# W_dec turned into contiguous tiles on chip, a new order of the setup, and splits in place in PSUM

## The chip, the cores and the metric

The kernel runs on one core of a Trainium2 chip. The metric is the device time of one execution in microseconds, the median of several runs. A core has five engines with a queue each: TensorE (PE in the profile, with its weight loads as PEld), VectorE (DVE), ScalarE (ACT), GpSimd (POOL) and SyncE (SP), which here only issues DMAs. Engines wait for each other through semaphores, and each works through its own list strictly in order.

## What is computed

Four conditioned layers, each added to its input, over x of 128 entries x 64 positions x 256 features in fp32 (cut to what matters):

```python
# layer 0: a weight per entry, decoded from its condition
U = (cond @ W_dec + b_dec).reshape(128, 257, 30)      # W_dec is 128 x 7710
x = x + (x @ (U[:, :-1] @ V) + U[:, -1] @ V)
# layer 1: modulated, demodulated product
s = cond @ (affine_w / sqrt(128)).T + affine_b
x = x + clip(((x * s) @ weight.T) * rsqrt(sum((weight * s)**2) + 1e-8) + bias, -256, 256)
# layer 2: adapter with weights made from the condition
x = x + (x + relu(x @ (down * dg + db)) @ (up * ug + ub))
# layer 3: norms with gains by class, three small nets, and an integration net
h = ln(ln(x, pw[id]), cp[id]);  t = ln(x, tm[id]);  s = ln(x, ms[id])
m, n, r = (x + ln(silu(c @ W1 + b1) @ W2 + b2) * g + be for c in three_conditions)
x = x + ln(silu(concat(softmax(aw) * [h, t, m, n, r, s]) @ int_W1 + b1) @ int_W2 + b2)
```

## The kernel before

**Setup.** The decode makes U: pe_dec (L447) runs 60 matmuls in 16 groups of four or two (GROUPS). Each takes one of the 30 columns r for 128 rows i out of wdec, whose elements lie in the order (i, r), so its weights are strided by 30 elements. v_decode (L542) adds b_dec and writes u_all. Six PSUM banks (dec_bank) serve in turn. pe_tail and v_ubias make the bias part, split it into three bf16 pieces, and act_ubwrite (L627) writes them to a scratch in DRAM, from which load_ub reads each chunk's part. pe_style, pe_dc, v_dceps, act_sqrt, v_dcrcp and g_dcoef make layer 1's coefficients. The three nets are pe_hid, act_hid (SiLU), pe_mo, v_mostat, g_moroot, v_monorm, pe_mot. pe_row and pe_cls then take them and the class biases through int_W1, and v_rows (L600) and v_classes (L606) split the results into bf16 pieces, all in SBUF; v_classes also picks each row's piece with masks. The loads of nets_W2, nets_rows and int_W1 reuse wdec and wait for the decode's last matmul.

**Main part.** Sixteen chunks of 512 positions (8 entries). For chunk c the stages are: act_u, pe_t, act_th1, act_th2, pe_x1, v_x1add (layer 0); g_style, pe_l1, v_l1mul, v_l1min, v_x2add (layer 1); pe_dn, v_dnmul, v_dnadd, act_relu, g_wup, pe_up, v_x3sum (layer 2, x3); pe_x3r, v_xstat, g_rootx, act_xnorm, pe_xht, act_xht (the norm); pe_tm, pe_ms, pe_cp with v_tmprod, v_msprod, v_hprod (gains by class); pe_shift and pe_w1_x3, _tm, _ms, _h (integration, in split precision), act_silu, act_silh, v_sillow, pe_w2, and the last norm v_ystat, v_ycentre, v_ynorm and store.

**Order.** Each engine has a list of (stage, chunk) written out by hand: begin, then a loop of ten rounds whose stages have fixed distances in chunks, then end. In the loop a round holds the integration of one chunk and the early layers of later ones:

```python
    for stage, n in begin:
        stage(eng, chunk(n))
    with eng.Fori(fill // 2, NCH // 2) as i:
        for k in range(2):
            for stage, lag in order:
```

The begin lists of before end ahead of chunk 0's pe_shift; the loop does the integration of chunks 0 to 9 and the end lists that of 10 to 15.

## Time and profile before

| | |
|---|---|
| median of 3 runs | 574.19 us (571.29 to 574.43) |
| the profiled execution: its own time | 574.62 us |
| its span, first to last instruction | 572.4 us |
| PE busy | 507.2 us, 89% |
| DVE, POOL, ACT busy | 80%, 69%, 52% |
| mean granted TensorE clock | 0.962 |

Times within a trace are us from the span's start. PE's granted clock is given as a share of 2.4 GHz; 0.50 is 1.2 GHz. A busy share over the whole span mixes the setup, the loop and the end, which have different limits.

### The profile page before, as it was taken

Reading aid. Unit: us, or ns where it says so; the run is one execution under the profiler, and the core shown is the slowest. Engines: PE = TensorE matmul, PEld = TensorE weight load, DVE = VectorE, ACT = ScalarE, POOL = GpSimd, SP = SyncE. Lnnn points to the kernel's source line nnn. Section 1 sums busy time; section 2 is a strip of 40 time slices with the busy share of each in tenths; the row PEclk is TensorE's granted clock in tenths of the full one; section 3 lists DMA queues with packets and bytes.
Section 4 is the critical chain, followed back from the end, with each engine's and each line's share of the span. In section 5 each row is a group of like instructions: output and inputs, shape, how many; then the busy total and the mean of one; then the engine's idle time right before and its main releaser. Section 6 shows DMA issues by size and latency. Waiting matters only on the chain.

```text
span 572.4 us, 8901 instructions
## 1 busy us (share of the span) xinstructions
PE 507.2 (89%) x2960; PEld 373.3 (65%) x2960; DVE 457.0 (80%) x857; ACT 299.6 (52%) x470; POOL 393.9 (69%) x382
## 2 busy tenths in 40 slices
PE   2996594699998999999999998999898999999873
PEld 2994252456767777677767776777666777778663
DVE  1444779768987898989898988898997989898833
ACT  0026424566647484848484848483746483656420
POOL 7601769288786788868886887688865897875320
PEclk9998787799998999999999999999999999999996
DMA  8338664033180808080908090908091505113011
GB/s 299 125 87 260 152 197 109 18 97 78 44 184 12 212 0 224 0 224 0 224 0 224 0 222 3 223 2 218 7 223 41 167 22 151 38 42 112 0 37 38
DMA packets 34955, 61.76 MB, mean 108 GB/s; under 512 B 4985, under 2 KB 17381, under 8 KB 34548
## 3 DMA queue, kind: packets, MB, share of 16 engines
q1 hardware_dynamic: 28868, 44.11, 28.5%
q0 software_dynamic: 5344, 16.87, 11.1%
q10 hardware_dynamic: 720, 0.48, 0.3%
q8 instruction: 13, 0.21, 0.2%
q14 instruction: 10, 0.08, 0.0%
HBM read 52.58 MB, written 8.87 MB: 107 GB/s over the span
## 4 chain that ended last, share of the span: by engine, by line
PE 60%; DMA 11%; DVE 9%; POOL 6%; issue 6%; SPq 3%; ACT 3%; POOLq 0%; DVEq 0%; ACTq 0%
PE ps_c L816 8%; PE ps_c L818 8%; PE ps_c L817 7%; DMA idx_ch<-in_mask 6%; PE ps_d L860 5%; PE ps_d L872 4%; PE ps_a L884 3%; PE ps_b L816 2%; PE ps_b L817 2%; PE ps_b L818 2%; DMA x_t<-in_x_t 2%; PE ps_a L456 2%; PE ps_b L902 2%; PE ps_c L456 2%; PE ps_a L902 2%
## 5 line engine op out<-in xcount | busy, mean ns | idle before, releaser
L1312 POOL DMA_INDIRECT pw_rows<-in_pw,gidx x64 | 71.2, 1112 | 27.9 <-issue 14.0
L860 PE MATMUL ps_d<-xm_t,l_w 128*128 128x512 f32 x128 | 60.9, 619 | 6.5 <-POOL xm_t L1321 6.5
L1321 POOL TENSOR_TENSOR xm_t<-x_t,style 128x1024 f32<-128x1024 f32 x16 | 30.5, 1905 | 38.8 <-DVE x_t L1163 38.8
L860 PEld LDWEIGHTS ps_d<-xm_t,l_w 128*128 128x128 f32 x128 | 23.8, 196 | 33.0 <-issue 30.7
L1350 POOL TENSOR_TENSOR h<-xhat,pw_rows 128x1024 f32<-128x1024 f32 x16 | 38.3, 2392 | 9.8 <-PE ps_b L902 6.8
L816 PE MATMUL ps_b<-w_h,act_t_l 128*128 128x256 f32 x128 | 40.8, 319 | 4.2 <-DVE act_t_l L1256 4.2
L1138 ACT ACTIVATE ps_c<-ps_c,bias_cols 128x512 f32<-128x512 f32 x32 | 19.8, 657 | 38.3 <-PE ps_c L818 38.2
L1380 POOL TENSOR_TENSOR x3be<-x,ln_gb 128x1024 f32<-128x1024 f32 x16 | 37.9, 2369 | 2.3 <-DVE y_out L1288 2.3
L1104 ACT ACTIVATE tm_t_h<-ps_a 128x1024 fp32r<-128x1024 f32 x16 | 16.4, 1027 | 43.7 <-DVE ps_a L1232 40.3
L1371 POOL TENSOR_TENSOR w_up<-w_up,ugub 128x1024 f32<-128x1024 f32 x16 | 38.2, 2385 | 1.3
L1355 POOL TENSOR_TENSOR h<-h,pw_rows 128x1024 f32<-128x1024 f32 x16 | 37.9, 2366 | 1.1
L1369 POOL TENSOR_TENSOR w_up<-up_rep,ugub 128x1024 f32<-128x1024 f32 x16 | 38.3, 2395 | 0.1
L817 PE MATMUL ps_b<-w_l,act_t_h 128*128 128x256 f32 x128 | 37.7, 295 | 0.0
L818 PE MATMUL ps_b<-w_h,act_t_h 128*128 128x256 f32 x128 | 37.7, 295 | 0.0
L872 PE MATMUL ps_d<-x_t,down_w 128*128 128x512 f32 x64 | 33.0, 642 | 4.7 <-DVE x_t L1185 4.7
L1116 ACT ACTIVATE ms_t_h<-ps_d 128x1024 fp32r<-128x1024 f32 x16 | 16.4, 1025 | 38.1 <-DVE ps_d L1237 38.0
L1074 ACT ACTIVATE xhat<-ps_a,nb_x,rstd_x 128x256 f32<-128x256 f32 x64 | 30.9, 566 | 9.5 <-POOL nb_x L1336 9.5
L1074 ACT ACTIVATE h<-h,nb_h,rstd_h 128x256 f32<-128x256 f32 x64 | 33.3, 603 | 4.3 <-POOL nb_h L1336 4.2
L1217 DVE BATCH_NORM_STATS2 bn_x<-ps_a 128x6 f32<-128x256 f32 x64 | 22.8, 419 | 14.6 <-PE ps_a L896 14.6
L884 PEld LDWEIGHTS ps_a<-act_bd,w_up 128*128 128x128 f32 x256 | 32.3, 199 | 3.1 <-DVE tm_t_l L1256 0.8
L884 PE MATMUL ps_a<-act_bd,w_up 128*128 128x128 f32 x256 | 32.9, 284 | 0.4 <-DVE tm_t_l L1256 0.3
L1217 DVE BATCH_NORM_STATS2 bn_y<-ps_b 128x6 f32<-128x256 f32 x64 | 22.7, 418 | 12.0 <-PE ps_b L818 12.0
(237 smaller groups left out, 1563.4 us busy)
## 6 DMA issues: line engine op xcount, KB each, us to landing
ugub<-ugub_scratch SPq DMA_DIRECT2D x32, 512.0 KB
x_t<-in_x_t SPq DMA_DIRECT2D x16, 512.0 KB, 9.2
out<-y_out SPq DMA_DIRECT2D x16, 512.0 KB, 4.4
set_wdec<-in_W_dec SPq DMA_DIRECT2D x2, 1920.0 KB, 9.6
set_wdec<-in_int_W SPq DMA_DIRECT2D x1, 1536.0 KB, 12.7
set_wdec<-in_nets_rows SPq DMA_DIRECT2D x1, 1152.0 KB, 6.9
pw_rows<-in_pw,gidx POOLq DMA_INDIRECT x64
set_wdec<-in_nets_W SPq DMA_DIRECT2D x1, 768.0 KB, 8.8
```

The source lines that it names most:

```text
L816: eng.matmul(out, wl, ah, start=first, stop=False)
L817: eng.matmul(out, wh, al, start=False, stop=False)
L818: return eng.matmul(out, wh, ah, start=False, stop=last)
L860: m = eng.matmul(ps_l1[:, o, :], l1_w[:, k, o * P:(o + 1) * P], xm_t[:, k, :], start=k == 0, stop=k == KB - 1)
L872: m = eng.matmul(ps_dn, down_w[:, k, :], x2_t[:, k, :], start=k == 0, stop=k == KB - 1)
L884: m = eng.matmul(ps_up[:, k, j * P:(j + 1) * P], w_up[:, j, k * P:(k + 1) * P], act_bd[:, j, :], start=True, stop=True)
L1074: m = eng.activation(out[:, j, :], src[:, j, :], ACT.Identity, bias=nb[k][:, j:j + 1], scale=rstd[k][:, j:j + 1])
L1217: m = eng.bn_stats(bn[k][:, j, :], src[:, j, :])
L1312: eng.indirect_dma_start(pw_rows[c.ring][:, j, :], None, t["pw"], bass.IndirectOffsetOnAxis(ap=gidx[c.ring][:, j:j + 1], axis=0)).then_inc ...
L1350: eng.tensor_tensor(h1[:, :, :], xhat[:, :, :], pw_rows[c.ring][:, :, 0:D], ALU.mult).then_inc(g_h1m, 1)
L1369: eng.tensor_tensor(w_up[:, :, :], q, ugub[:, :, 0:D], ALU.mult).then_inc(g_upm, 1)
L1371: eng.tensor_tensor(w_up[:, :, :], w_up[:, :, :], ugub[:, :, D:2 * D], ALU.add).then_inc(g_up, 1)
```

## The change

- A ring of eight tiles w_rt is added. A group's part of wdec is copied into one of them in the order (r, i), so that the matmul's weights are contiguous. Every third group is copied by VectorE (v_turn), the others by ScalarE (act_turn); pe_dec waits for the copy instead of for the load.
- The front load goes second in SP's list; the loads of l1_wt, nets, weights, int_W1, nets_W2 and nets_rows have new places.
- ScalarE's order is Exp, Sqrt, SiLU, where it was Sqrt, SiLU, Exp.
- The splits of the bias part, the rows and the classes work in place in PSUM (split_in_place), without copies in SBUF. The classes' split and pick are joined through a small table (later), which v_gains makes with two instructions of one column each. The nets' norm also works in place, in ps_c in place of ps_a.
- The begin lists now hold chunk 0 through pe_w2 and the store, and the loop's distances are one less throughout, so that it does chunks 1 to 10; the end lists start one chunk later and are reordered.
- Waits of pe_ms, pe_hht, g_gather, g_hmul, act_x3 and others on setup steps are changed to fit.

The diff, cut to its core (lists shortened where "..." stands, their indentation too):

```diff
@@ -370,11 +372,21 @@
             link(eng.scalar_tensor_tensor(r1, p2, masks[:, 1:2], r1, ALU.mult, ALU.add))
             return eng.scalar_tensor_tensor(out, p3, masks[:, 2:3], r1, ALU.mult, ALU.add)
 
+        def split_in_place(eng, link, src, p1, p2, p3):
+
+            link(eng.tensor_copy(p1, src))
+            link(eng.tensor_tensor(src, src, p1, ALU.subtract))
+            link(eng.tensor_copy(p2, src))
+            link(eng.tensor_tensor(src, src, p2, ALU.subtract))
+            link(eng.tensor_copy(p3, src))
+
         v_link = chain(nc.vector, v_chain)
         g_link = chain(nc.gpsimd, g_chain)
+        V_TURN = [g for g in range(NG) if g % 3 == 2]
+        A_TURN = [g for g in range(NG) if g % 3 != 2]
...
@@ -447,13 +459,13 @@
         def pe_dec(eng, c):
             g = c.n
             k, lo, hi = GROUPS[g]
-            if lo == 0:
+            if g == 0:
                 eng.wait_ge(d_front, 32)
-                eng.wait_ge(d_dec[k], 16)
             wait(eng, v_dec, g - len(dec_bank) + 1)
-            w = wdec[:, k * P * RK:(k + 1) * P * RK].rearrange("m (i r) -> m r i", r=RK)
-            for r in range(lo, hi):
-                m = eng.matmul(dec_bank[g % 6][:, (r - lo) * B:(r - lo + 1) * B], w[:, r, :], mu, start=True, stop=True)
+            mine, s = (V_TURN, v_rt) if g in V_TURN else (A_TURN, c_rt)
+            eng.wait_ge(s, mine.index(g) + 1)
+            for r in range(hi - lo):
+                m = eng.matmul(dec_bank[g % 6][:, r * B:(r + 1) * B], w_rt[:, g % RING, r, :], mu, start=True, stop=True)
             m.then_inc(m_dec, 1)
...
@@ -534,10 +545,19 @@
             eng.wait_ge(z_pad, len(pads))
             eng.wait_ge(m_tail, 1)
             eng.wait_ge(d_bdec, 32)
-            v_link(eng.tensor_tensor(ubias[0][:, :], ps_b[:, 1, 0:RK], bdec_u[:, :], ALU.add))
-            split(eng, v_link, ubias[0][:, :], ubias[1][:, :], ubias[2][:, :],
-                  *(ubias_p[:, e * RP:e * RP + RK] for e in range(PIECES)))
+            v_link(eng.tensor_tensor(ps_b[:, 1, 0:RK], ps_b[:, 1, 0:RK], bdec_u[:, :], ALU.add))
+            split_in_place(eng, v_link, ps_b[:, 1, 0:RK], *(ubias_p[:, e * RP:e * RP + RK] for e in range(PIECES)))
             eng.sem_inc(v_ub, 1)
+
+        def turned(eng, g):
+            k, lo, hi = GROUPS[g]
+            eng.wait_ge(d_dec[k], 16)
+            wait(eng, m_dec, g - RING + 1)
+            w = wdec[:, k * P * RK:(k + 1) * P * RK].rearrange("m (i r) -> m r i", r=RK)
+            return w_rt[:, g % RING, 0:hi - lo, :], w[:, lo:hi, :]
+
+        def v_turn(eng, c):
+            eng.tensor_copy(*turned(eng, c.n)).then_inc(v_rt, 1)
...
@@ -579,9 +599,9 @@
         def v_mostat(eng, c):
             eng.wait_ge(m_mo, 1)
             eng.wait_ge(d_rown, 16)
-            v_link(eng.tensor_tensor(mo[1][:, :, :], rows_a[:, 0:3, :], rown[:, :, 0, :], ALU.add))
+            v_link(eng.tensor_tensor(rows_c[:, 0:3, :], rows_c[:, 0:3, :], rown[:, :, 0, :], ALU.add))
             for n in range(3):
-                last = eng.bn_stats(mo_bn[:, n, :], mo[1][:, n, :])
+                last = eng.bn_stats(mo_bn[:, n, :], rows_c[:, n, :])
...
-                last = eng.tensor_scalar(mo[0][:, n, :], mo[1][:, n, :], mo_mv[:, n, 0:1], mo_r[:, n:n + 1],
+                last = eng.tensor_scalar(rows_c[:, n, :], rows_c[:, n, :], mo_mv[:, n, 0:1], mo_r[:, n:n + 1],
                     ALU.subtract, ALU.mult)
             v_link(last)
-            v_link(eng.tensor_tensor(mo[1][:, :, :], mo[0][:, :, :], rown[:, :, 1, :], ALU.mult))
-            eng.tensor_tensor(mo[0][:, :, :], mo[1][:, :, :], rown[:, :, 2, :], ALU.add).then_inc(v_mo, 1)
+            v_link(eng.tensor_tensor(rows_c[:, 0:3, :], rows_c[:, 0:3, :], rown[:, :, 1, :], ALU.mult))
+            eng.tensor_tensor(mo[:, :, :], rows_c[:, 0:3, :], rown[:, :, 2, :], ALU.add).then_inc(v_mo, 1)
...
         def v_rows(eng, c):
             eng.wait_ge(m_row, 1)
-            v_link(eng.tensor_copy(rowb[0][:, :], ps_c[:, 0, 0:D]))
-            split(eng, v_link, rowb[0][:, :], rowb[1][:, :], rowb[2][:, :], *(rowb_p[:, e, :] for e in range(PIECES)))
+            split_in_place(eng, v_link, ps_c[:, 0, 0:D], *(rowb_p[:, e, :] for e in range(PIECES)))
             eng.sem_inc(v_row, 1)
 
         def v_classes(eng, c):
             eng.wait_ge(m_cls, 1)
-            eng.wait_ge(d_gain, 64)
+            eng.wait_ge(v_pick, 1)
             eng.wait_ge(z_pad, len(pads))
-            v_link(eng.tensor_copy(clsb[0][:, :], ps_c[0:CLS, 1, 0:D]))
-            pieces = [p[:, :] for p in clsb_p]
-            split(eng, v_link, clsb[0][:, :], clsb[1][:, :], clsb[2][:, :], *pieces)
-            pick(eng, v_link, shift[0][0:CLS, :], clsb[1][:, :], *pieces).then_inc(v_cls, 1)
+            src = ps_c[0:CLS, 1, 0:D]
+            for e in range(PIECES - 1):
+                v_link(eng.tensor_copy(clsb_p[e][:, :], src))
+                v_link(eng.scalar_tensor_tensor(src, clsb_p[e][:, :], later[:, e:e + 1], src, ALU.mult, ALU.add))
+            eng.tensor_copy(shift[0][0:CLS, :], src).then_inc(v_cls, 1)
...
+        def act_turn(eng, c):
+            out, src = turned(eng, c.n)
+            eng.activation(out, src, ACT.Copy).then_inc(c_rt, 1)
...
-            wait(eng, v_h, c.n)
+            newest(eng, c, (v_h, -1), (v_x2, 1), (v_msl, -1))
...
-            wait(eng, v_y, c.n)
+            newest(eng, c, (v_y, -1), (v_x1, 2), (v_hl, -1))
+            newest(eng, c, (v_y, -1), (a_th1, 3), (v_x1, 2), (v_hl, -1))
...
-    begin=[(load_dec, 0), (load_bdec, 0), (load_aw, 0), (load_l1, 0), (load_front, 0),
-        (load_dec, 1), (load_x, 0), (load_side, 0), (load_ident, 0), (load_entry, 0),
-        (load_bias, 0), (load_late, 0), (load_ub, 0), (load_ub, 1), (load_nets, 0),
-        (load_ids, 0), (load_weights, 0), (load_x, 1), (load_rown, 0), (load_w2n, 0),
-        (load_w1, 0), (load_up, 0), (load_ids, 1), (load_ub, 2), (load_up, 1), (load_ub, 3),
-        (load_x, 2), (load_up, 2), (load_x, 3), (load_ub, 4), (load_shift, 0)],
+    begin=[(load_dec, 0), (load_front, 0), (load_bdec, 0), (load_aw, 0), (load_dec, 1),
+        (load_x, 0), (load_bias, 0), (load_ident, 0), (load_nets, 0), (load_side, 0),
+        (load_entry, 0), (load_x, 1), (load_ub, 0), (load_l1, 0), (load_ub, 1),
+        (load_ids, 0), (load_weights, 0), (load_late, 0), (load_w1, 0), (load_up, 0),
+        (load_ub, 2), (load_w2n, 0), (load_ids, 1), (load_rown, 0), (load_x, 2),
+        (load_up, 1), (load_shift, 0), (load_ub, 3), (load_ids, 2), (load_up, 2),
+        (load_ub, 4), (load_x, 3), (load_up, 3), (load_ub, 5), (load_x, 4), (load_shift, 1),
...
-    begin=[(pe_dec, 0), (pe_dec, 1), (pe_dec, 2), (pe_dec, 3), (pe_dec, 4), (pe_dec, 5),
-        (pe_dec, 6), (pe_tail, 0), (pe_dec, 7), (pe_dec, 8), (pe_dec, 9), (pe_dec, 10),
-        (pe_style, 0), (pe_dec, 11), (pe_dec, 12), (pe_dec, 13), (pe_dec, 14), (pe_dec, 15),
-        (pe_dc, 0), (pe_hid, 0), (pe_ug, 0), (pe_t, 0), (pe_mo, 0), (pe_x1, 0), (pe_l1, 0),
-        (pe_mot, 0), (pe_t, 1), (pe_dn, 0), (pe_row, 0), (pe_up, 0), (pe_x1, 1), (pe_x3r, 0),
-        (pe_cls, 0), (pe_l1, 1), (pe_t, 2), (pe_xht, 0), (pe_tm, 0), (pe_dn, 1), (pe_ms, 0),
...
+    begin=[(pe_dec, 0), (pe_tail, 0), (pe_dec, 1), (pe_dec, 2), (pe_dec, 3), (pe_dec, 4),
+        (pe_dec, 5), (pe_dec, 6), (pe_dec, 7), (pe_dec, 8), (pe_dec, 9), (pe_dec, 10),
+        (pe_dec, 11), (pe_dec, 12), (pe_style, 0), (pe_dec, 13), (pe_dec, 14), (pe_dec, 15),
+        (pe_ug, 0), (pe_t, 0), (pe_dc, 0), (pe_x1, 0), (pe_hid, 0), (pe_t, 1), (pe_l1, 0),
+        (pe_mo, 0), (pe_dn, 0), (pe_up, 0), (pe_x1, 1), (pe_x3r, 0), (pe_mot, 0), (pe_t, 2),
+        (pe_l1, 1), (pe_row, 0), (pe_cls, 0), (pe_dn, 1), (pe_xht, 0), (pe_tm, 0),
+        (pe_ms, 0), (pe_x1, 2), (pe_up, 1), (pe_shift, 0), (pe_w1_x3, 0), (pe_x3r, 1),
+        (pe_l1, 2), (pe_w1_tm, 0), (pe_t, 3), (pe_cp, 0), (pe_xht, 1), (pe_hht, 0),
+        (pe_tm, 1), (pe_dn, 2), (pe_w1_ms, 0), (pe_ms, 1), (pe_up, 2), (pe_x1, 3),
...
-    begin=[(act_ubwrite, 0), (act_style, 0), (act_w2high, 0), (act_u, 0), (act_dg, 0),
-        (act_sqrt, 0), (act_hid, 0), (act_exp, 0), (act_u, 1), (act_th1, 0), (act_ug, 0),
-        (act_th2, 0), (act_w1scale, 0), (act_mot, 0), (act_onehot, 0), (act_u, 2),
...
+    begin=[(act_turn, 0), (act_turn, 1), (act_turn, 3), (act_turn, 4), (act_turn, 6),
+        (act_turn, 7), (act_exp, 0), (act_ubwrite, 0), (act_turn, 9), (act_turn, 10),
+        (act_turn, 12), (act_turn, 13), (act_turn, 15), (act_style, 0), (act_u, 0),
+        (act_dg, 0), (act_ug, 0), (act_th1, 0), (act_th2, 0), (act_u, 1), (act_sqrt, 0),
+        (act_th1, 1), (act_hid, 0), (act_u, 2), (act_w2high, 0), (act_th2, 1),
+        (act_w1scale, 0), (act_relu, 0), (act_x3h, 0), (act_onehot, 0), (act_th1, 2),
+        (act_mot, 0), (act_u, 3), (act_th2, 2), (act_w1high, 0), (act_onehot, 1),
+        (act_x3, 0), (act_xnorm, 0), (act_xht, 0), (act_rowwrite, 0), (act_shift, 0),
...
-    begin=[(v_pads, 0), (v_decode, 0), (v_decode, 1), (v_decode, 2), (v_awmax, 0),
-        (v_decode, 3), (v_decode, 4), (v_decode, 5), (v_ubias, 0), (v_decode, 6),
-        (v_decode, 7), (v_decode, 8), (v_l1sq, 0), (v_decode, 9), (v_decode, 10),
-        (v_decode, 11), (v_decode, 12), (v_stylesq, 0), (v_decode, 13), (v_decode, 14),
-        (v_decode, 15), (v_dceps, 0), (v_gains, 0), (v_dcrcp, 0), (v_mostat, 0),
-        (v_x1add, 0), (v_monorm, 0), (v_softmax, 0), (v_l1mul, 0), (v_l1min, 0),
-        (v_x2add, 0), (v_w1sum, 0), (v_dnmul, 0), (v_dnadd, 0), (v_rows, 0), (v_x3sum, 0),
...
+    begin=[(v_pads, 0), (v_turn, 2), (v_turn, 5), (v_awmax, 0), (v_decode, 0), (v_ubias, 0),
+        (v_decode, 1), (v_decode, 2), (v_decode, 3), (v_decode, 4), (v_decode, 5),
+        (v_turn, 8), (v_turn, 11), (v_turn, 14), (v_decode, 6), (v_decode, 7), (v_decode, 8),
+        (v_decode, 9), (v_decode, 10), (v_decode, 11), (v_decode, 12), (v_decode, 13),
+        (v_decode, 14), (v_decode, 15), (v_stylesq, 0), (v_l1sq, 0), (v_gains, 0),
+        (v_dceps, 0), (v_x1add, 0), (v_dcrcp, 0), (v_softmax, 0), (v_l1mul, 0), (v_l1min, 0),
+        (v_x2add, 0), (v_mostat, 0), (v_dnmul, 0), (v_dnadd, 0), (v_monorm, 0), (v_x3sum, 0),
+        (v_x1add, 1), (v_xstat, 0), (v_w1sum, 0), (v_x3low, 0), (v_l1mul, 1), (v_l1min, 1),
+        (v_x2add, 1), (v_rows, 0), (v_classes, 0), (v_dnmul, 1), (v_dnadd, 1), (v_tmprod, 0),
+        (v_msprod, 0), (v_tmlow, 0), (v_x3sum, 1), (v_x1add, 2), (v_hstat, 0), (v_mslow, 0),
...
-    begin=[(g_init, 0), (g_b2rows, 0), (g_w2low, 0), (g_dcoef, 0), (g_moroot, 0), (g_style, 0),
-        (g_gather, 0), (g_wup, 0), (g_gather, 1), (g_style, 1), (g_rootx, 0), (g_w1mlow, 0),
...
+    begin=[(g_init, 0), (g_b2rows, 0), (g_style, 0), (g_dcoef, 0), (g_wup, 0), (g_w2low, 0),
+        (g_moroot, 0), (g_gather, 0), (g_style, 1), (g_gather, 1), (g_rootx, 0), (g_wup, 1),
+        (g_w1xlow, 0), (g_hmul, 0), (g_hadd, 0), (g_w1tlow, 0), (g_w1mlow, 0), (g_style, 2),
...
-    order=[(load_x, 2), (load_up, 3), (load_shift, 5), (load_ids, 4), (load_ub, 1), (store, 6)],
+    order=[(load_x, 1), (load_up, 2), (load_shift, 4), (load_ids, 3), (load_ub, 0), (store, 5)],
+    end=[(load_x, 15), (load_up, 14), (load_ids, 13), (load_ids, 14), (load_shift, 12),
...
```

## Rows read from the trace of the kernel before

**Rows 1.** Page, 40 slices of the span in tenths, and one group
```profile
PE   2996594699998999999999998999898999999873
...
PEclk9998787799998999999999999999999999999996
...
L884 PE MATMUL ps_a<-act_bd,w_up 128*128 128x128 f32 x256 | 32.9, 284 | 0.4 <-DVE tm_t_l L1256 0.3
```

**Rows 2.** Stretches: start:end and length, busy us (instructions) by engine, clock, DMA share, GB/s
```profile
11.40:42.20 30.80, 30.34 (x128) 30.15 (x128) 13.69 (x26) 2.43 (x4) 13.60 (x17) 1.00 0.41 135
42.20:117.90 75.70, 51.12 (x301) 29.52 (x302) 54.99 (x86) 37.61 (x67) 42.89 (x37) 0.82 0.51 144
58.50:65.00 6.50, 3.65 (x5) 1.62 (x6) 5.69 (x9) 0.39 (x1) 5.30 (x5) 0.50 0.71 138
117.90:403.00 285.10, 277.03 (x1701) 200.97 (x1700) 251.97 (x466) 176.59 (x271) 224.82 (x207) 0.99 0.44 109
403.00:572.40 169.40, 148.74 (x833) 112.72 (x831) 134.60 (x271) 83.00 (x128) 105.09 (x103) 0.96 0.26 74
```

**Rows 3.** Lines, 11 to 43 us: busy us, mean ns, idle before and its releaser
```profile
L456 PEld LDWEIGHTS ps_a<-set_mu,set_wdec 128*128 128x128 f32 x44 | 11.0, 340 | 11.4 <-DMA set_wtail<-in_W_dec 11.4
...
L548 DVE TENSOR_TENSOR u_all<-ps_a,set_bdec 128x512 f32<-128x512 f32 x5 | 3.5, 692 | 14.7 <-PE ps_a L456 14.5 <-DVE set_ubias_p L364 0.2
...
L1028 ACT ACTIVATE u_ch<-u_all 128x480 f32<-128x480 f32 x1 | 1.0, 1045 | 8.1 <-DVE u_all L548 8.1
...
L477 PEld LDWEIGHTS ps_a<-set_style,set_wsq 128*128 128x128 f32 x7 | 0.9, 191 | 0.7 <-DVE u_all L548 0.7
```

**Rows 4.** Timeline of PE, 40 to 44 us: start, length, instructions
```profile
42.27 1.16 PE L477 MATMUL ps_a<-set_style,set_wsq 128*128 128x128 f32 x8 [0.52 <-DVE u_all L548]
43.27 0.61 PE L488 MATMUL ps_c<-set_mu,set_w_mem 128*128 128x128 f32 x4
```

**Rows 5.** DMA issues at 0.7 and at 42.6 us: KB, us to landing
```profile
set_wdec<-in_W_dec SPq DMA_DIRECT2D x1, 1920.0 KB, 7.9
...
set_wdec<-in_int_W SPq DMA_DIRECT2D x1, 1536.0 KB, 12.7
```

**Rows 6.** Timeline of ACT, 25 to 60 us
```profile
27.94 2.38 ACTq L630 DMA_DIRECT2D ub_scratch<-set_ubias_p  x3
...
48.18 1.28 ACT L635 ACT_TABLE_LOAD   x1
...
50.49 1.10 ACT L1036 ACTIVATE t_st<-ps_b 30x128 f32<-30x128 f32 x4
51.62 0.60 ACT L652 ACTIVATE set_ugub_row<-ps_d 128x512 f32<-128x512 f32 x1
52.24 0.37 ACTq L654 DMA_DIRECT2D ugub_scratch<-set_ugub_row  x1
```

**Rows 7.** Timeline of PE, 50 to 118 us
```profile
51.08 4.51 PE L498 MATMUL ps_a<-set_wdec,set_hid 128*128 128x256 f32 x12 [4.23 <-DMA set_wdec<-in_nets_W]
...
61.35 5.57 PE L860 MATMUL ps_d<-xm_t,l_w 128*128 128x512 f32 x8 [4.70 <-POOL xm_t L1321]
...
114.22 3.67 PE L860 MATMUL ps_d<-xm_t,l_w 128*128 128x512 f32 x8 [1.26 <-POOL xm_t L1321]
```

**Rows 8.** Chain of waits that ended last, 40 to 118 us
```profile
59.33 1.88 POOL xm_t L1321
...
67.03 1.24 DVE ps_d L1170
...
71.19 2.95 PE ps_d L872 x4
```

**Rows 9.** Timeline of DVE, 85 to 95 us
```profile
85.88 0.41 DVE L361 TENSOR_TENSOR set_clsb<-set_clsb,set_clsb_p 24x256 f32<-24x256 f32 x1
...
87.76 2.47 DVE L363 TENSOR_TENSOR set_clsb<-set_clsb,set_clsb_p 24x256 f32<-24x256 f32 x1
```

**Rows 10.** Timeline of PE, 425 to 435 us
```profile
431.64 0.65 PE L833 MATMUL ps_b<-x_t,u_ch 128*30 128x64 f32 x32 [2.28 <-DMA x_t<-in_x_t]
```

208 lines of the change are left out of this document (100 added, 108 removed).

## The prediction

> **What bounds the kernel now.** I read the page first: the slices show where TensorE is not full, in the first eight and the last two [rows 1]. Then the stretches: from 117.9 to 403 us, the ten rounds of the loop, TensorE works 277 of 285 us at a granted clock of 0.99, so that part is bound by it and a reordering has little to win there [rows 2]. Two stretches are different. From 11.4 to 42.2 the decode of W_dec occupies TensorE completely, and from 42.2 to 117.9 it is busy 51.1 of 75.7 us at a mean clock of 0.82. So the setup is the place to look. The last 169.4 us lose 20.7 us, about half of it after the last matmul.
>
> The lines of the decode say why it is slow: the weights are strided by 30 elements and their loads take 340 ns, where the contiguous ones of L477 take 191 [rows 3]. The eight contiguous records of L477 start at 42.27 and the next line at 43.27, 0.125 us each [rows 4]; the 120 of the decode take 30.3 us, 0.253 each [rows 2]. TensorE's timeline then shows what follows: the nets' product, held 4.2 us for its weights, the first l1 product at 61.35, the third at 114.2 [rows 7]. In between VectorE spends 10 us on the classes, in instructions of 24x256 that take 0.41 us when undisturbed and up to 2.47 us beside POOL's long ones [rows 9].
>
> **The change part by part: the decode.** TensorE's 60 matmuls fall from 30.3 to 120 x 0.125 = 15.0 us, but each of 16 groups now waits for a turned copy, 11 on ScalarE and 5 on VectorE. No row shows this copy. The nearest is ScalarE's u_ch copy, also strided in its source: 1.04 us for 480 elements, so 1.1 us for 512 [rows 3]. The bounds are 0.6 us (a contiguous copy of 512 takes 0.60 [rows 6]) and 2.2 us (twice the strided row); I take 1.1, as TensorE's strided loads show the same kind of surcharge.
>
> The start moves forward too. TensorE waited until 11.4 for the tail's load, issued behind five others; W_dec's first half had landed at 0.74 + 7.9 = 8.6 [rows 5], and the front load now goes second. ScalarE's sum: 8.6, 11 turns 12.1, Exp with its table load 1.5, the three ub writes 2.4 [rows 6], together 24.6, and the last group's matmuls, add and one more VectorE step behind it: 27. The ub writes wait for the bias split, which needs only the first decode add and is over at about 14, before Exp. VectorE's sum: 8.6, five turns 5.5, 16 adds of 0.69 [rows 3] 11.0, split and maximum 2.4: 27.5. So the last add ends at 27.5, against 42.2 now: **-14.7 us**. At the turns' lower price it is 25, at the upper one ScalarE ends at 36.7 and the decode at 39: a gain between 3 and 17.
>
> VectorE's subtraction of 24x256 took 2.47 us beside POOL's work and 0.41 alone [rows 9]. Five turns that each wait so long, 2.1 us more, would put up to 10 us on VectorE's sum; POOL's splits are over by then in part, so I take nothing and keep 5 us for the range. The Trainium skill, SBUF — State Buffer, section "SBUF: two separate sides", says that GpSimd and a VectorE instruction in a two-port mode, or with two SBUF inputs, shut each other out for whole instructions; by that rule, the trace agrees, the VectorE turns can queue behind POOL's splits and the new splits with a PSUM source can't.
>
> **From the decode to the first integration product.** I follow chunk 0 in the new order from 27.5. VectorE takes 0.69 us for 512 columns [rows 3] and 1.24 for 1024 [rows 8]; steps whose rows aren't shown are matmul groups of about 1 us.
> - u copy 1.04, pe_t, then th1 (1.10) behind the eviction and DMA issue of ugub (0.60 and 0.4 [rows 6]), th2, x1, x1 add 1.2, style 1.9 [rows 8]: 36.4. Before, these ended at 61.3, because TensorE took the nets' product ahead of x1, 4.2 us of wait and 4.5 of work [rows 7], and VectorE their statistics ahead of the add. Sqrt ahead of SiLU keeps only part of a table load of 1.28 away from here [rows 6].
> - l1 3.7 [rows 7]; multiply, clamp and x2 from 67.03 to 71.1, 4.0 [rows 8]: 44.1. POOL's coefficients are ready at 39.5.
> - The nets: their weights and rows now come behind W1 and the first ugub, issued from 27 on. Three loads of 3.5 MB took until 12.7 us after the last issue [rows 5]; with 1 MB more the rows land near 46.5. v_mostat stands ahead of v_dnmul on VectorE, so this is a **new wait** of some 2 us; behind it are dnmul and dnadd, and relu and up wait for them. 46.5 + 2.4 (statistics) + 2.1 (three of 0.69) + relu 0.9 + up 2.1 (32.9 / 16 [rows 1]) = 54.0. monorm, in PSUM, lies beside relu and up.
> - x3sum, x1 add, style 4.4, second l1 3.7, x2 4.0: 66.1. Rows and classes are ten short PSUM instructions of 0.4: 70.1. xh copy and gains 1.6, then dn's and the products' VectorE work 2.1 + 3 x 1.24, up(1): pe_shift(0) starts near 79.
> Handovers of 0.1 us for some 35 steps add 3.5 and two stretches at half clock 3: 85.5. After the 4.7 us in which TensorE waited for xm_t [rows 7], the stretch from 58.5 to 65.0 was at 0.50, that is 1.2 GHz [rows 2], and the eight l1 records took 5.6 us, not 3.7 [rows 7]; the new order still has such gaps, before up(0) and before the gains. Without them, -3; with all of the present ones (75.7 us at 0.82), +6.
> The same point before is 117.9 less the work that the new order does after it (third l1 3.7, pe_x3r and pe_t 2.0): 112.2. The difference is 26.7, so this stretch gives **-12.0 us** beyond the decode.
>
> **The rest.** The loop's ten rounds keep order and distances, and the waits rewritten in pe_ms and pe_hht are the same there: 0. The end lists keep the last chunk's chain. x(14) is now issued in the loop, and the 2.28 us for which TensorE waited for it [rows 10] may go; I take -1, between +3 (one misplaced stage) and -4.
> Sum on the profiled execution: span 572.4 - 14.7 - 12.0 - 1 = 544.7. Its own time is 574.6, 2.2 more, so 546.9; the median of the runs is 0.4 below that execution. I say 547.
>
> **Rivals.**
> - *Only the decode's gain survives* (15%): x1, relu or the products wait for the late W1, ugub or rows, with SP standing in front of load_up or load_shift. For it: the loads that three needed 12.7 us for are now four [rows 5]. Against it: the present gaps are mostly waits of order. 547 + 12 = 559.
> - *The turn is dear* (10%), 2.2 us each; the decode ends at 39, the rest as forecast: 547 + 11.5 = 558.5. The Trainium skill, SBUF — State Buffer, section "Door 1: The DMA port swizzle", says in a box that each access to a new 16-byte line pays, which speaks against the change: the surcharge goes from TensorE to the copying engines; the trace's 1.04 us agrees.
> - *The setup packs better than I follow it* (12%): no half clock, handovers hidden, the end gives 4: 547 - 3 - 4 - 3 = 537.
> - *Slower* (4%): a load late in every round. store(0) now stands at the end of SP's hand-written list, and each store's wait is ahead of the next x. The 2.28 us for x [rows 10] occur once; in each of 15 rounds they would cost 34 us: 581. It decides from 26.7 / 15 = 1.8 us a round. Against it: the loop loses 8 us in ten rounds [rows 2].
>
> **How the numbers follow.** The forecast has 59%, with 541 to 553 as its own range (turn's price, clock, end). With the other cases 537 to 561 holds eight in ten. A measurement of this kernel can tell about 0.5%, 2.9 us, from no change. Faster takes all cases but the slower rival and mixtures of two bad ones: 0.93; same 0.03; slower 0.04.
>
> **What would show it.** Decode: matmul records of 0.125 us, last u_all add at 26 to 31. Turn: ScalarE rows of 128x512 at 1.1 us. Classes: five instructions under 0.5 us each. Setup: first l1 product at 36 to 40, pe_shift(0) at 80 to 90, mean clock above 0.82. Loop: the same time a round. I am wrong if the turns take over 1.5 us, if VectorE waits over 5 us for the nets' rows, or if a round gets longer.

## The result, and the profile after

The changed kernel takes 544.83 us (median of 4 runs, 543.65 to 547.78), the kernel before 573.52 us on the same chip (571.29 to 574.43): ratio 0.951, 95% interval 0.946 to 0.956. The forecast was 547, and the range 537 to 561. The profiled execution of the changed kernel is its slowest run, 547.78 us with a span of 545.7. The same kernel was run once more, called `after_again` below; its profiled execution has a span of 543.5 us.

The page of the changed kernel, TensorE's slices and its granted clock, beside [rows 1]:

```profile
span 545.7 us, 8914 instructions
...
PE   2985688899999999999999999999999999989773
...
PEclk9977897999999999999999999999999999999896
```

The dip at the start is shorter and shallower, and it is still there. The stretches say where, to be read beside [rows 2]: start:end and length, busy us (instructions) by engine, granted clock, DMA share, GB/s.

```profile
9.60:27.10 17.50, 16.76 (x128) 16.40 (x128) 13.87 (x28) 10.40 (x13) 14.10 (x17) 1.00 0.75 249
27.10:88.00 60.90, 44.89 (x252) 27.41 (x253) 39.71 (x65) 31.93 (x58) 37.41 (x32) 0.81 0.61 170
35.90:42.20 6.30, 6.24 (x8) 2.33 (x8) 0.62 (x2) 6.18 (x15) 2.50 (x4) 0.59 0.54 137
42.20:58.00 15.80, 6.18 (x16) 4.12 (x16) 9.25 (x17) 4.24 (x8) 7.89 (x7) 0.78 0.87 244
155.30:411.30 256.00, 252.68 (x1568) 183.85 (x1567) 232.53 (x442) 152.66 (x246) 203.82 (x190) 1.00 0.44 113
```

The decode's 128 records take 17.5 us instead of 30.8. Then TensorE works 6.2 of 15.8 us between 42.2 and 58.0. The loop runs at full clock. ScalarE's and VectorE's timelines of the decode, in two pieces (start, length, instructions, and in brackets the idle time before them with its releaser):

```profile
8.28 6.01 ACT L652 ACTIVATE set_w_rt<-set_wdec 128x512 f32<-128x512 f32 x6 [6.26 <-DMA set_wdec<-in_W_dec]
...
14.18 0.20 ACT L662 ACTIVATE set_aw_s<-set_aw_s 128x6 f32<-128x6 f32 x1
...
16.09 5.00 ACT L652 ACTIVATE set_w_rt<-set_wdec 128x512 f32<-128x512 f32 x5 [1.71 <-DMA set_wdec<-in_W_dec]
```

```profile
8.28 1.20 DVE L560 COPY set_w_rt<-set_wdec 128x512 f32<-128x512 f32 x2 [5.63 <-DMA set_wdec<-in_W_dec]
...
18.06 2.47 DVE L560 COPY set_w_rt<-set_wdec 128x512 f32<-128x512 f32 x3
...
26.05 1.02 DVE L568 TENSOR_TENSOR u_all<-ps_c,set_bdec 128x512 f32<-128x512 f32 x2 [0.20 <-PE ps_c L468]
```

A turn (the copy of one group into a tile of w_rt) costs ScalarE 1.0 us and VectorE 0.6 us, the last three on VectorE 0.8. Exp is there without a table load. The last u_all add ends at 27.07.

What sets that end is TensorE. From its first matmul at 9.60 it works 16.8 of 17.5 us, and VectorE's adds wait for it, 0.2 us before nearly each. Its records are not of one length. Two stretches of the decode:

```profile
9.60:13.70 4.10, 4.10 (x19) 4.10 (x20) 2.18 (x8) 4.10 (x5) 2.55 (x3) 1.00 1.03 412
13.80:26.10 12.30, 12.21 (x109) 12.04 (x109) 10.62 (x18) 6.21 (x9) 10.46 (x13) 1.00 0.67 202
```

The first 19 records come 0.22 us apart and the next 109 come 0.11 us apart, so the first ones cost 2 us more than they would at the later pace. The view prints a clock of 1.00 for both, but the clock records of this trace begin only at 13.8. TensorE's timeline shows the rest of the setup, beside [rows 7], and SP's queue why it has its gap:

```profile
35.89 6.25 PE L887 MATMUL ps_d<-xm_t,l_w 128*128 128x512 f32 x8 [0.31 <-POOL xm_t L1345]
48.01 4.46 PE L509 MATMUL ps_c<-set_wdec,set_hid 128*128 128x256 f32 x12 [5.87 <-DMA set_wdec<-in_nets_W]
52.31 1.88 PE L899 MATMUL ps_d<-x_t,down_w 128*128 128x512 f32 x4
58.03 3.65 PE L911 MATMUL ps_a<-act_bd,w_up 128*128 128x128 f32 x16 [3.85 <-ACT act_bd L1081]
...
87.97 1.04 PE L994 MATMUL ps_c<-onehot,shift 128*128 128x512 bf16 x2
```

```profile
26.93 0.43 SPq L446 DMA_DIRECT2D set_wdec<-in_int_W  x1
36.91 1.55 SPq L832 DMA_DIRECT2D ugub<-ugub_scratch  x2
...
39.05 0.39 SPq L437 DMA_DIRECT2D set_wdec<-in_nets_W  x1
...
40.52 0.80 SPq L441 DMA_DIRECT2D set_wdec<-in_nets_rows  x1
```

SP issues W1 at 26.9 and then stands for 10 us at the first ugub, whose write to the scratch, issued at 28.97, takes 7.9 us to land. Behind it the nets' weights are issued at 39.05 and land at 47.9.

**A yardstick through the kernel.** pe_shift occurs once a chunk. Where the setup hands over to the loop the two orders differ: between pe_shift(0) and pe_shift(1) the changed kernel does work that the kernel before has behind it, 38.3 us against 28.9. From pe_shift(1) on the work done is the same: ahead of it both traces have 601 matmul records. Start of pe_shift for chunks 0, 1, 2 and 10, and the span, read from each trace:

```
                  0      1      2     10    span
before          117.7  146.6  179.0  409.6  572.4
splits_before   111.6  140.3  172.9  400.6  564.3
turn_before     107.5  136.2  166.1  394.1  557.7
both_before     101.0  129.7  159.4  388.1  546.8
strided_after    96.9  135.2  163.3  389.9  552.8
after            88.0  126.2  155.3  382.3  545.7
after_again      87.1  125.4  153.3  381.9  543.5
w1_last          82.0  120.2  148.7  376.1  539.9
```

### The profile page after: what moved, and what is told of

It reads as the page before. It is cut to its first block, busy times and chain, and to the rows that moved or that the text cites. A ratio compares the mean times of both kernels' runs of the same rounds, so it can differ in the third digit from the quotient of the medians.

```text
span 545.7 us, 8914 instructions
## 1 busy us (share of the span) xinstructions
PE 492.7 (90%) x2960; PEld 359.3 (66%) x2960; DVE 450.2 (83%) x859; ACT 295.6 (54%) x470; POOL 394.4 (72%) x382
## 4 chain that ended last, share of the span: by engine, by line
PE 52%; DVE 15%; DMA 13%; POOL 6%; issue 5%; ACT 4%; SPq 4%; POOLq 0%; DVEq 0%; ACTq 0%
DMA idx_ch<-in_mask 9%; PE ps_c L843 7%; PE ps_c L845 7%; PE ps_c L844 7%; PE ps_d L887 4%; PE ps_a L911 3%; PE ps_d L899 3%; PE ps_b L843 2%; PE ps_b L845 2%; PE ps_b L844 2%; PE ps_b L929 2%; POOL w_up L1394 2%; DVE y_out L1316 2%; DMA set_wdec<-in_nets_W 2%; PE ps_b L875 2%
## 5 line engine op out<-in xcount | busy, mean ns | idle before, releaser
L887 PE MATMUL ps_d<-xm_t,l_w 128*128 128x512 f32 x128 | 61.7, 626 | 2.4 <-DVE ms_t_l L1284 1.2
L1394 POOL TENSOR_TENSOR w_up<-up_rep,ugub 128x1024 f32<-128x1024 f32 x16 | 38.3, 2393 | 7.7 <-DMA ugub<-ugub_scratch 7.2
L887 PEld LDWEIGHTS ps_d<-xm_t,l_w 128*128 128x128 f32 x128 | 23.9, 197 | 28.9 <-issue 25.1
L911 PEld LDWEIGHTS ps_a<-act_bd,w_up 128*128 128x128 f32 x256 | 33.8, 208 | 10.8 <-issue 4.6
L911 PE MATMUL ps_a<-act_bd,w_up 128*128 128x128 f32 x256 | 35.0, 295 | 5.6 <-ACT act_bd L1081 3.8
L1101 ACT ACTIVATE xhat<-ps_a,nb_x,rstd_x 128x256 f32<-128x256 f32 x64 | 30.8, 566 | 5.9 <-POOL nb_x L1360 5.9
L843 PEld LDWEIGHTS ps_b<-w_h,act_t_l 128*128 128x128 f32 x128 | 25.3, 198 | 8.7 <-DVE act_t_l L1284 7.1
L899 PE MATMUL ps_d<-x_t,down_w 128*128 128x512 f32 x64 | 30.2, 594 | 0.0
## 6 DMA issues: line engine op xcount, KB each, us to landing
set_wdec<-in_int_W SPq DMA_DIRECT2D x1, 1536.0 KB, 11.2
```

Source lines behind the costliest of these rows:

```text
L843: eng.matmul(out, wl, ah, start=first, stop=False)
L887: m = eng.matmul(ps_l1[:, o, :], l1_w[:, k, o * P:(o + 1) * P], xm_t[:, k, :], start=k == 0, stop=k == KB - 1)
L899: m = eng.matmul(ps_dn, down_w[:, k, :], x2_t[:, k, :], start=k == 0, stop=k == KB - 1)
L911: m = eng.matmul(ps_up[:, k, j * P:(j + 1) * P], w_up[:, j, k * P:(k + 1) * P], act_bd[:, j, :], start=True, stop=True)
L1101: m = eng.activation(out[:, j, :], src[:, j, :], ACT.Identity, bias=nb[k][:, j:j + 1], scale=rstd[k][:, j:j + 1])
L1394: eng.tensor_tensor(w_up[:, :, :], q, ugub[:, :, 0:D], ALU.mult).then_inc(g_upm, 1)
```

## The experiments

Each kernel was timed against the kernel before on its chip, and its ratio is given with the 95% interval. The changed kernel's, to compare with, is 0.952 (0.949 to 0.956), from `after_again`. Differences in us are differences of ratios times 573.5. An interval of 0.005 to either side is 3 us, so such a difference is known to some 3 or 4 us.

> The changed kernel itself once more, so that the kernels of this set have it on the same chip. All theories: 544.8 us, 542 to 548, ratio 0.951.

Measured: 545.76 us.

**turn_before**, the turns alone in the kernel before:

```
+    w = wdec[...].rearrange("m (i r) -> m r i", r=RK)
+    return w_rt[:, g % RING, 0:hi - lo, :], w[:, lo:hi, :]     # copied by ScalarE (11) or VectorE (5)
-    eng.matmul(dec_bank[...], w[:, r, :], mu, ...)
+    eng.matmul(dec_bank[...], w_rt[:, g % RING, r, :], mu, ...)
     SP: (load_dec, 0), (load_front, 0), ...; TensorE: (pe_dec, 0), (pe_tail, 0), ...
```

> The kernel before with one part of the change alone: W_dec's groups turned by ScalarE (11) and VectorE (5), front load second, tail product second; all orders behind the decode stay as before, and the splits too. Theory (decode and new order are separate gains that add): the decode ends near 28 instead of 42.2, time 573.5 - 13 = 560, range 558 to 562. Rival: in the old order the nets' weights, W1 and rows, which wait for the end of the decode, have no more time to land; TensorE waits for them and part of the gain is lost: 564 to 568.

Ratio 0.978 (0.973 to 0.983), 12.7 us. The decode ends at 31.0, 11.2 us earlier, and pe_shift(0) is 10.2 us earlier, so almost the whole gain arrives; the nets' product waits 4.0 us for its weights, as before. 2.5 us more come between pe_shift(1) and pe_shift(2), 29.8 instead of 32.4 us. TensorE's timeline of the kernel before, not yet shown, has a wait there, and its clock is halved behind it:

```profile
174.17 0.81 PE L1011 MATMUL ps_b<-b_row,ones 128*128 128x512 bf16 x2 [2.72 <-ACT t_st L1036]
```

```profile
174.40:177.80 3.40, 3.40 (x17) 3.31 (x16) 1.52 (x2) 3.38 (x7) 3.32 (x2) 0.50 0.00 0
```

With the turns the wait is 1.7 us and the clock behind it stays at 1.00. The theory holds; the rival loss did not occur.

The decode ends 3.9 us later here than in the changed kernel, and the trace shows why: the bias split is still made in SBUF. VectorE's timeline:

```profile
14.65 1.51 DVE L367 TENSOR_TENSOR set_ubias<-set_ubias,set_ubias_p 128x30 f32<-128x30 f32 x1
```

This instruction, beside one of POOL's splits (14.43 to 16.11), takes 1.51 us, and the same step in PSUM 0.20 us in the changed kernel. The whole split takes 4.5 us instead of 1.3, VectorE's last three turns come 2.1 us later, TensorE waits 2.0 us for the first of them and then runs 3.4 us at half clock. So the split in place is part of what the decode gains in the changed kernel; no run has it alone.

**strided_after**, the changed kernel without the turns:

```
-    (act_turn, 0) ... (act_turn, 15), (v_turn, 2) ... (v_turn, 14)
-    eng.matmul(dec_bank[...], w_rt[:, g % RING, r, :], mu, ...)
+    eng.matmul(dec_bank[...], w[:, r, :], mu, ...)             # w strided by 30, as before
```

> The changed kernel with one part undone: TensorE reads the strided W_dec itself again, nothing is turned; all orders and the other edits stay. Theory (the turn itself earns the decode's gain): the 120 matmuls take 0.25 us each, 30 us instead of 15, and the decode ends near 42 instead of 27, 14 to 15 us later. If everything behind it moves along: 544.8 + 14 = 559, range 557 to 561. Rival A: the front load's earlier place earns 2 to 3 us of the decode, which stays: then the decode ends at 39 to 40 and the time is 556 to 557. Rival B: the setup behind the decode is held by loads, not by the decode's end: then part of the 14 us is hidden and the time is 550 or less.

Ratio 0.975 (0.970 to 0.981): 13 us lost against 0.952. In the trace the decode ends at 40.0, 13 us later than with the turns and 2 us earlier than in the kernel before: rival A is right, the earlier front load earns those 2 (the first matmul starts at 9.0 instead of 11.4). At pe_shift(1) 8.9 us are left, because 3.8 us of the nets' gap were hidden behind the longer decode, in part what rival B had expected:

```profile
57.01 4.51 PE L509 MATMUL ps_c<-set_wdec,set_hid 128*128 128x256 f32 x12 [2.10 <-DMA set_wdec<-in_nets_W]
```

Trace and medians differ by 4 us here; this execution was the fastest of its four.

**turn_unit**, the price of the stride:

```
-    w = wdec[...].rearrange("m (i r) -> m r i", r=RK)
+    flat = wdec[...].rearrange("m (r i) -> m r i", i=P)        # source contiguous
```

> The changed kernel, but the turning copies read W_dec with unit stride, so that what they hold is not the turned weights: the same instructions, shapes and orders, and another U than the reference's is computed. It prices the stride. Theory (the stride is the copy's surcharge, as the contiguous 128x512 copy on ScalarE takes 0.63 us): ScalarE's turns take 0.63 instead of 1.0 us, VectorE's 0.35 to 0.45 instead of 0.6; the first half gets 2 us shorter, the second begins when W_dec's second half has landed near 16, and the last add ends at 24.5 to 25.5 instead of 27.1; the time falls by 1.5 to 2.5 us, to 543. Rival: VectorE's 16 adds and the landing of the second half already set the decode's end: 27 and 545.

Timelines of ScalarE and of VectorE:

```profile
8.17 3.01 ACT L653 ACTIVATE set_w_rt<-set_wdec 128x512 f32<-128x512 f32 x6 [6.15 <-DMA set_wdec<-in_W_dec]
...
15.95 2.19 ACT L653 ACTIVATE set_w_rt<-set_wdec 128x512 f32<-128x512 f32 x4 [3.83 <-DMA set_wdec<-in_W_dec]
```

```profile
17.93 1.76 DVE L561 COPY set_w_rt<-set_wdec 128x512 f32<-128x512 f32 x3
...
25.69 1.02 DVE L569 TENSOR_TENSOR u_all<-ps_c,set_bdec 128x512 f32<-128x512 f32 x2 [0.20 <-PE ps_c L468]
```

ScalarE's turn takes 0.50 us instead of 1.00, so the stride doubles it. That is the rule from which the rival of the dear turn was built (the Trainium skill, SBUF — State Buffer, "Door 1: The DMA port swizzle": an access to a new 16-byte line pays), and the runs agree with it, by a factor of two. But the decode ends at 26.7 instead of 27.1, and the ratio is 0.955 (0.950 to 0.959): the rival's numbers are right, its reason is not. ScalarE only waits longer for W_dec's second half (3.8 us instead of 1.7), and VectorE's adds wait for TensorE as before. The chain of waits runs through TensorE's matmuls, from 8.99 to 25.7 here and from 9.60 to 26.0 in the changed kernel: they start 0.6 us earlier, but now 23 records are slow instead of 19. So the cheaper turn is worth at most half a microsecond of the decode, and the times show no gain. (In this one execution, the fastest of its four, pe_shift(0) comes at 84.9, 2 to 3 us ahead of the changed kernel's; there the first l1 product ran at full clock, 3.67 us instead of 6.25, and the ugub's write landed in 7.0 us instead of 7.9. Whether that follows from the cheaper turn was not tested.)

**splits_before**, rows and classes split in place in the kernel before:

```
-    v_link(eng.tensor_copy(clsb[0][:, :], ps_c[0:CLS, 1, 0:D]))
-    split(eng, v_link, clsb[0], clsb[1], clsb[2], *pieces)
-    pick(eng, v_link, shift[0][0:CLS, :], clsb[1][:, :], *pieces)
+    for e in range(PIECES - 1):
+        v_link(eng.tensor_copy(clsb_p[e][:, :], src))
+        v_link(eng.scalar_tensor_tensor(src, clsb_p[e][:, :], later[:, e:e + 1], src, ALU.mult, ALU.add))
+    eng.tensor_copy(shift[0][0:CLS, :], src)
```

> The kernel before with one part of the change alone: rows and classes are split in place in PSUM by the new short forms (five instructions each), with the small table of factors that this needs. Theory (the classes' 9.7 us, stretched beside POOL's work, hold the second l1 multiply): they take 2.3 us and the multiply starts at 88.8, when TensorE is done, instead of 94.8: 573.5 - 6 = 567.5, range 566 to 569. Rival: the wait is only given to the next instruction (the xh copy and gains product come from POOL's and ScalarE's chain), or POOL's contention moves to the next two-source instructions: 571 to 573.5.

VectorE's timeline, where [rows 9] had 2.47 us for one instruction:

```profile
84.89 0.41 DVE L620 CAST set_clsb_p<-ps_c 24x256 bf16<-24x256 f32 x1 [0.72 <-PE ps_c L533]
85.34 0.48 DVE L621 SCALAR_TENSOR_TENSOR ps_c<-set_clsb_p,later,ps_c 24x256 f32<-24x256 bf16 x1
...
86.81 0.41 DVE L622 CAST shift<-ps_c 24x256 bf16<-24x256 f32 x1
88.52 1.23 DVE L1181 TENSOR_TENSOR ps_d<-ps_d,dcoef 128x1024 f32<-128x1024 f32 x1 [1.30 <-PE ps_d L871]
```

The classes take 2.3 us instead of 9.7, and the second l1 multiply starts 6.3 us earlier, when TensorE is done with the product. POOL's instruction of 1.3 us, beside which the kernel before had its 1.4 us cast, now runs beside them from 85.95 on, and they stay at 0.41 and 0.48. pe_shift(0) is 6.1 us earlier, as forecast. The ratio, 0.984 (0.978 to 0.990), says 9.2 us, more than the forecast's 4.5 to 7.5, but its interval reaches down to 5.7; in the trace 3 us more come between pe_shift(2) and pe_shift(10), where the kernel before was slow (230.6 us, see below).

**both_before**, the two together in the kernel before, whose orders stay.

> The kernel before with two parts of the change, the turned W_dec and the in-place splits of rows and classes; all orders behind the decode stay as before. Alone they gave ratios of 0.978 and 0.984. Theory (the parts add, and the new orders of the setup earn what is left): ratio 0.962, about 551.5 us at 573.2 for the kernel before, and the first integration product at 101.5 instead of 117.7. Rival A: the classes' stretch depends on what POOL does beside them, which the earlier decode shifts, so that the parts overlap: ratio 0.967 to 0.972, 554 to 557. Rival B: the new orders earn nothing of their own, and these two parts are all: ratio 0.952, 546.

pe_shift(0) comes at 101.0, the forecast 101.5, so the two gains, 10.2 and 6.1 us, add there. The ratio is 0.956 (0.951 to 0.962), 25 us, more than the sum of the two; it holds all but 2.3 us of the changed kernel's 27.3, and the intervals overlap. So the new orders earn little in the time, although at pe_shift(2) the changed kernel stands 4.1 and 6.1 us ahead (155.3 and 153.3 against 159.4), of which 2.5 us are its decode's earlier end (27.1 against 29.6). Part of the difference is lost at the very end. Behind pe_shift(10) `both_before` took 158.7 us, the changed kernel 163.4 and 161.6. Its x wait was 0.95 us instead of [rows 10]'s 2.28, and its last product kept the clock, after the same wait for act_t_l. Two 8 us stretches behind that wait, first of `both_before`, then of the kernel before:

```profile
534.00:542.00 8.00, 3.11 (x24) 2.90 (x24) 4.58 (x16) 0.00 (x0) 1.22 (x2) 0.84 0.00 0
```

```profile
557.00:565.00 8.00, 5.49 (x24) 5.20 (x24) 2.24 (x10) 0.00 (x0) 0.00 (x0) 0.59 0.01 2
```

The same 24 matmuls take 3.1 us in the one and 5.5 in the other. `both_before` has the same steps behind the loop as the kernel before, so this is not the change's doing; whether it keeps the clock there as a rule was not settled.

**exp_late** and **old_end**, two smaller parts undone: Exp behind the nets' SiLU on ScalarE, and the end lists of all engines in the old order.

```
     exp_late, on ScalarE:
-    (act_turn, 7), (act_exp, 0), (act_ubwrite, 0), ... (act_hid, 0), (act_u, 2)
+    (act_turn, 7), (act_ubwrite, 0), ... (act_hid, 0), (act_exp, 0), (act_u, 2)
     old_end, on TensorE (the other four engines likewise):
-    end=[(pe_xht, 12), (pe_shift, 11), (pe_w1_x3, 11), (pe_cp, 11), ...]
+    end= the same steps, in the sequence that they have in the kernel before
```

> The changed kernel with Exp back behind the nets' SiLU on ScalarE, so that the decode has no table load in it and a third one stands at about 39.7 instead. Theory (as predicted, it matters little: ScalarE has 11 us of slack ahead of relu(0), and the decode is held by W_dec's second half and VectorE): 544.8 within 1 us. Rival A: the decode gets 1.4 us shorter without it and all moves along: 543. Rival B: v_softmax stands ahead of the first l1 multiply on VectorE and now waits for Exp: 546 to 547.

> The changed kernel with the end lists of all five engines in the order of the kernel before (the same steps, the loop and the setup unchanged). Theory, as predicted: the end earned about 1 us (the wait for x is in the loop now either way): 545 to 547. Rival A: the new end order earns more, 3 to 4 us: 548 to 549. Rival B: the new end order has cost something, since the trace of the changed kernel shows new waits of 2.8 and 3.3 us for act_t_l and half-clock stretches behind them that the kernel before does not have: 541 to 543.

Ratios 0.955 (0.952 to 0.958) and 0.954 (0.950 to 0.957) against 0.952 in the same set: neither is told from no change. In `exp_late` the extra table load of 1.28 us stands at 40.6, in ScalarE's slack; pe_shift(0) is at 86.8 against 87.1. Its decode, with Exp out of it, did not get shorter (it ends at 28.4), as TensorE sets its end. In `old_end` the stretch behind pe_shift(10) takes 163.6 us. Its expectation is wrong in one thing: the kernel before does have the 3.3 us wait for act_t_l and a half-clock stretch behind it (the second of the two stretches above); only the 2.8 us wait is new.

**nets_first, w1_last and nets_behind**: can the gap at 42.2 to 58.0 be closed?

```
 SP, changed:      w1, up(0), ub(2), w2n, ids(1), rown, x(2)
 SP, nets_first:   w2n, rown, w1, up(0), ub(2), ids(1), x(2)
 SP, w1_last:      w2n, up(0), rown, w1, ub(2), ids(1), x(2)   ScalarE: (act_relu, 0), (act_w1scale, 0)
 nets_behind:      w1_last, and (v_mostat, 0) behind (v_dnadd, 0), (v_monorm, 0) behind (v_x1add, 1),
                   (pe_mot, 0) behind (pe_l1, 1), (act_mot, 0) behind (act_w1high, 0)
```

> The changed kernel with SP's loads behind the decode in another order: the nets' W2 and rows ahead of W1, the first ugub and the third ub. Theory (the 5.9 us for which TensorE waits for the nets' weights and VectorE and dn behind it are a gap on the path): the nets' product starts at 42.5 instead of 48.0 and the time falls by 4 to 6 us, to 539 to 541. Rival: the first ugub then comes later and w_up holds up(0), or W1 holds the rows and classes: the gap moves, and the time stays within 1.5 us of 544.8.

TensorE's timeline. The nets' product starts 7 us earlier, and the gap is now at w_up (up's weights), whose ugub comes behind W1; ratio 0.957 (0.953 to 0.961), no gain, rather a loss of 3 us. My theory fell, its rival held:

```profile
40.84 2.75 PE L509 MATMUL ps_c<-set_wdec,set_hid 128*128 128x256 f32 x12
...
56.34 3.75 PE L911 MATMUL ps_a<-act_bd,w_up 128*128 128x128 f32 x16 [9.11 <-POOL w_up L1396]
```

> The changed kernel with SP's loads behind the decode as nets' W2, first ugub, nets' rows, W1, third ub, and ScalarE's scaling of W1 behind relu(0) and not ahead of it. The run with W1 last but the ugub behind it had shown that the nets' product then starts 7 us earlier and that the gap moves to w_up, 9.1 us. Theory (the gap is only the order of three loads; with the small ugub ahead of W1 nothing on the path waits for a load): up(0) starts near 51 instead of 58.0, no wait over 3 us ahead of it, and the time is 5 to 7 us less: 538 to 540. Rival: the ugub's write to the scratch lands only when the loads ahead of it have, about 8 to 10 us after its issue, and SP then holds the rows behind it: up(0) starts at 55 or later and the time is 543 to 546.

(The earlier run that this refers to is `nets_first`, in which W1 stands behind the nets' loads and ahead of the ugub.)

```profile
40.69 2.75 PE L509 MATMUL ps_c<-set_wdec,set_hid 128*128 128x256 f32 x12
45.13 1.95 PE L899 MATMUL ps_d<-x_t,down_w 128*128 128x512 f32 x4 [1.68 <-DVE x_t L1213]
52.16 3.52 PE L911 MATMUL ps_a<-act_bd,w_up 128*128 128x128 f32 x16 [5.08 <-ACT act_bd L1081]
```

up(0) starts 5.9 us earlier, pe_shift(0) is at 82.0, and the ratio is 0.945 (0.942 to 0.949): 4 us less than `after_again` by the ratios, 3.4 by the medians (542.35 and 545.76), and no run of the one reaches a run of the other. No load holds TensorE itself now. The 5 us ahead of up(0) are VectorE's: 1.7 us of waiting for the nets' rows, then the statistics and dn.

> The version of the changed kernel with the ugub ahead of the nets' rows and of W1 (540.3 to 543.1 us there), and besides it the nets' statistics behind dnadd(0), their norm behind the second x1 add, and their transposes behind the second l1 product. Theory (the statistics, 1.7 us of wait for the rows and 2.4 of work, stand on the path to up(0)): VectorE's dnmul starts at 47.2 instead of 49.0, up(0) at 50 instead of 52.2, bounded by w_up, ready at 48.7; nets' norm lies beside the second l1; ratio 0.942 after 0.945, 540 us. Rival: the 2 us are given back where TensorE waits for the nets' transposes, their copy and the rows behind the second l1: within 1 us of 542.4.

up(0) does start at 50.5, but the ratio is 0.951 (0.946 to 0.955), the gain is gone. It was lost on an engine that neither theory named. POOL's and TensorE's timelines:

```profile
51.87 0.20 POOL L760 TENSOR_SCALAR set_mo_ve<-set_mo_mv 128x3 f32<-128x3 f32 x1 [2.99 <-DVE set_mo_mv L607]
...
54.09 1.13 POOL L1336 DMA_INDIRECT pw_rows<-in_pw,gidx  x1 [0.90 <-POOL gidx L1332]
...
59.01 1.91 POOL L1345 TENSOR_TENSOR xm_t<-x_t,style 128x1024 f32<-128x1024 f32 x1
```

```profile
60.98 2.08 PE L887 MATMUL ps_d<-xm_t,l_w 128*128 128x512 f32 x2 [3.51 <-POOL xm_t L1345]
```

The later statistics hold g_moroot, the first gathers stand behind it in POOL's order, and g_style(1) behind those: the second l1 waits 3.5 us and then runs at half clock, 5.1 us for 3.7.

**keep_busy**: `w1_last` with work for TensorE in the two last waits.

```
-    for k in range(KB):
-        eng.matmul(ps_y[:, k, :], ones[:, :], b2_row[:, :], start=True, stop=False)
+    times = {14: 6, 15: 7}.get(c.n, 1) if isinstance(c.n, int) else 1
+    for n in range(times):
+        for k in range(KB):
+            eng.matmul(ps_y[:, k, :], ones[:, :], b2_row[:, :], start=True, stop=n < times - 1)
     wait(eng, v_sill, c.n + 1)
```

> The version with the ugub ahead of the nets' rows and of W1 (540.3 to 543.1 us), and in the last two chunks the two bias matmuls at the head of the output product are repeated, 5 and 6 more pairs, so that TensorE works while it would wait for act_t_l (2.8 and 3.3 us there). They write the same values again. In that version's trace each wait is followed by 1.2 us of matmuls at full clock, then 3.3 us at half clock, in which 16 matmuls of 128x256 take 0.21 us apart instead of 0.12. Theory (the half clock follows from the wait): both half-clock stretches go, 1.5 us each, and the time is 3 us less, 539 to 540; the last product's 24 matmuls take 3.1 us instead of 5.5. Rival: the granted clock falls there whatever TensorE does, or the short bf16 matmuls don't hold it: within 1 us of 542.4. Second rival: the repeats outlast the waits and delay both products: 543 to 544.

Stretches of `w1_last` behind the two waits, and then of `keep_busy` at the same products:

```profile
505.90:509.10 3.20, 3.20 (x17) 3.10 (x15) 1.23 (x1) 0.37 (x1) 0.00 (x0) 0.50 0.00 0
...
526.40:529.60 3.20, 3.20 (x18) 3.20 (x17) 0.00 (x0) 0.00 (x0) 0.00 (x0) 0.50 0.02 5
```

```profile
507.50:510.40 2.90, 2.90 (x24) 2.90 (x24) 2.30 (x2) 1.54 (x4) 0.00 (x0) 1.00 0.00 0
526.80:530.00 3.20, 3.11 (x24) 2.91 (x24) 0.05 (x1) 0.00 (x0) 0.00 (x0) 1.00 0.00 0
```

Both half-clock stretches are gone, which answers the first rival for this kernel; the first product of each pair still starts 3.4 and 3.6 us behind its first bias matmul, as in `w1_last` (3.4 and 3.9), so the repeats delay nothing. From its first bias matmul the chunk 14 product takes 6.4 us instead of 7.8 (504.1 to 510.5 against 501.3 to 509.1), and the last one, up to its last matmul's end, 6.7 instead of 8.5: 3.2 us. The time is 540.54 us, ratio 0.943 (0.939 to 0.948), the best of all kernels here, but from 0.945 it is not told apart by the medians; its profiled setup was 0.6 us and its stretch to pe_shift(1) 1.4 us slower, which hides part of the 3.2.

## Why the prediction was right, and where its steps were not

The sum was right to 1 us on the profiled execution (544.7 forecast, 545.7 and 543.5 measured), and the two things that it built on, contiguous weights and short splits, do what it said. That it was so close is luck: the setup gave 6 us less than forecast, and the part behind it 5 us more.

- **The decode, -14.7: measured -15.1** (last add 27.07 against 42.2). The size held, and so did the price of a ScalarE turn (1.0 us for the 1.1 taken) and its start (8.3 for 8.6). The path did not. The sum ended on VectorE (27.5) with ScalarE close by (27), and it was TensorE that set the end: it started at 9.60 and its 128 records took 0.128 us each on average, 0.22 at first and 0.11 later, for the 0.125 taken; ScalarE's last turn was over at 21.1. Two terms were off without effect. Exp needed no table load: the first Copy loads one at 0.74, in idle time, and at 14.18 Exp takes 0.20 us alone, 1.3 of the 3.5 us by which ScalarE's 24.6 was too long. The Trainium skill, ScalarE: Activation LUTs, section "Table sets: the hidden batching unit", says that cheap functions such as copy are in every set; the trace agrees. And VectorE's turns were cheaper (0.6) but for the three beside POOL (0.8). The runs show what the decode is worth in the time: 12.7 us in the old order, with the earlier front load, and 13 in the new, without it, each within some 3 us.
- **From the decode to pe_shift, -12.0: measured -5.3 at pe_shift(1)** (146.6 - 126.2 = 20.4, less 15.1). This is the step that failed, in two terms. First the correction for work that the new order does behind pe_shift(0) was taken as 5.7 us of matmuls; it is 9.3 us with its waits (38.3 against 28.9 us to the next pe_shift). Second, "a new wait of some 2 us" for the nets' rows on VectorE was mis-sized and on the wrong load. The sum had the four loads "issued from 27 on", but SP stood at the first ugub until 36.9, for its scratch write, with the nets' W2 behind it. TensorE waited 5.9 us for W2, VectorE 6.3 for the product, and the first l1 and the product ran at half clock (6.25 and 4.5 us). up(0) was to end at 54.0 and ended at 61.7. My own test had asked for over 5 us of VectorE's waiting for the nets' rows: it waited 6.3 us at that place, though for the product, as the rows had landed at 50.9. By its sense the test came out against me.
- **What cancelled it.** From the end of up(0) to pe_shift(0) the sum had 31.5 us, with 6.5 for handovers and half clock; it took 26.3, about the 25.0 that it had without those 6.5; the half clock had come ahead of up(0). And the rest gave more than -1: TensorE's wait for t_st between pe_shift(1) and (2), 2.7 us in the kernel before, shrank to 1.0 and the half clock behind it went (together 3.3 us), and eight rounds of the loop took 227.0 and 228.6 us instead of 230.6. The other three kernels in the old order took 227.7 to 228.7, so most of this last part belongs to that one execution of the kernel before, and no term of the sum foresaw either.
- **Splits, which I had inside the 12 us:** 6.1 us at pe_shift(0), by the experiment. The trace of `splits_before` has them short beside POOL (0.41 and 0.48 us). By the rule cited for it (the Trainium skill, SBUF — State Buffer, "SBUF: two separate sides") POOL can shut out a VectorE instruction that is in a two-port mode or has two SBUF inputs, and the in-place steps read a source from PSUM; the trace agrees.
- **The end, -1:** TensorE's wait for x is gone, and waits for act_t_l grew from 4.2 to 6.1 us; pe_shift(10) to the end takes 163.4 and 161.6 us, before 162.8. The order of the end is worth nothing that the runs can tell.
- **Rivals.** "Only the decode survives" named the right culprit, SP standing in front of load_up, and overrated it: it costs what `w1_last` gets back, 4 us, not 12. The dear turn is refuted (1.0 us, not 2.2), and `turn_unit` shows that a turn at half its price does not shorten the time either. The slower case did not come.

In all: turns and front load 12.7 us, the splits of rows and classes 6 to 9, and the new orders with the rest 2 to 6. The rest holds the bias split in place, which was not run alone and goes with a decode that ends 2.5 us earlier than in `both_before`. For the orders only the trace at pe_shift(2) says that they earn anything, 1.6 and 3.6 us beyond the decode; their share of the final time stays open within about 3 us.

## What to carry to other kernels

Before costing a new order of loads, follow the one queue that issues them: an instruction that waits for a write to land holds every load behind it. Here another order of four loads around such a wait was worth 4 us: the nets' weights, the small ugub and the nets' rows ahead of the 1.5 MB W1, with ScalarE's use of W1 moved back to match. Compare two orders at a point where the same work is done, and check the correction by the interval to the next such point. A cheaper instruction is worth something only where its engine sets the end: look at what it waits for once it is faster, and follow the chain of waits to see which engine does. When a sum comes out right, check its terms at points in between: here a shortfall of 6 us and a surplus of 5 hid each other.

## What the runs showed of the hardware

- A strided source costs the copying engine too: ScalarE's 128x512 f32 copy at a stride of 30 elements takes 1.00 us, contiguous 0.50. TensorE's weight loads at that stride took 340 ns and contiguous ones 191 [rows 3]; from start to start that is 0.25 and 0.11 us.
- The first 19 matmul records of the changed kernel's trace (23 in `turn_unit`) came 0.22 us apart, the next ones 0.11; the trace shows no wait among them.
- A wait of 2.8 or 3.3 us at the end of the kernel was mostly followed by half clock (in 7 of 8 traces and in 12 of 13, `keep_busy` left out), but not always. In `w1_last` TensorE ran about 1 us at 2.4 GHz behind each, then 3.4 us at 1.2, and then again at 2.4. In the kernel before it was at 1.2 GHz from the first matmul on, and the last 24 matmuls took 5.5 us. The clock held twice: in `both_before` behind the 3.3 us wait, where the same 24 took 3.1 us, and in `after_again` behind the 2.8 us wait. Ten and twelve short bf16 matmuls in the waits kept it at 2.4 in the one execution of `keep_busy` that was traced. These 2.4 us are part of what sets one execution apart from another. The stretch of `after_again` behind the 2.8 us wait:

```profile
510.13:513.10 2.97, 2.97 (x25) 2.93 (x26) 2.30 (x2) 1.55 (x4) 0.00 (x0) 1.00 0.00 0
```

- An in-place split in PSUM kept its length beside POOL's work (0.20 us a step), the same step in SBUF took up to 1.51 us.
- A 256 KB write to DRAM took 7.9 us to land when it was issued 2 us behind a 1.5 MB load, and 5.7 us in `w1_last`, where a load of 0.77 MB was ahead of it.
